# Four-layer conditional residual kernel on one core: W0 in four row quarters, added to and turned quarter by quarter

## What is computed

```
x = x + x @ W.T + ((x @ A[idx0].T) @ Bm[idx0].T) * scal[idx0]   # layer 0, a matrix and a rank-16 adapter per sequence
x = x + per-sequence mix of the tokens with w1[idx1]            # layer 1, 64 x 64
x = x + causal attention(x, beta = min(cond, 4)), 16 heads      # layer 2, Wq Wk Wv Wo
x = x + per-sequence mix of the tokens with w3[idx3]            # layer 3, 64 x 64
```

## Time and profile before

| | before |
|---|---|
| median of three runs | 611.03 us (610.99 to 611.15) |
| the profiled execution: time | 610.91 us |
| its span, first to last instruction | 609.2 us, 21490 instructions |
| TensorE busy | 601.7 us (99%) |
| VectorE busy | 392.9 us (64%) |
| ScalarE busy | 224.8 us (37%) |
| GpSimd busy | 109.8 us (18%) |
| mean granted TensorE clock | 0.997 |
| chain of work that ended last | PE 95%, DVE 4%, issue 1% |

### The profile page before, as it was taken

The page is one execution under the profiler, slowest core; times in us unless marked ns, Lnnn a source line. Parts: engine busy times, 40 slices in busy tenths (PEclk is TensorE's granted clock), DMA queues, the critical chain, the costliest instruction groups (busy, mean ns, idle before and its releaser), DMA issues.

```text
span 609.2 us, 21490 instructions
## 1 busy us (share of the span) xinstructions
PE 601.7 (99%) x8524; PEld 521.0 (86%) x8524; DVE 392.9 (64%) x573; ACT 224.8 (37%) x434; POOL 109.8 (18%) x101
## 2 busy tenths in 40 slices
PE   9999999899999999999999999999999999999998
PEld 8898889788898988889888898988889898888885
DVE  4699865665657567575775657567575766647374
ACT  4555351342524334251442424344251443513222
POOL 2003120301203031040401204040030302103030
PEclk9999999899999999999999999999999999999999
DMA  9962322222222322223222322322222231320212
GB/s 292 173 130 66 87 56 75 74 63 74 71 64 80 93 71 62 73 60 78 73 65 73 86 74 57 88 73 61 74 64 73 74 79 59 65 72 3 71 41 104
DMA packets 65272, 48.29 MB, mean 79 GB/s; under 512 B 16922, under 2 KB 51738, under 8 KB 65242
## 3 DMA queue, kind: packets, MB, share of 16 engines
q1 hardware_dynamic: 60090, 42.63, 26.7%
q10 hardware_dynamic: 5152, 5.24, 3.0%
HBM read 30.54 MB, written 17.30 MB: 79 GB/s over the span
## 4 chain that ended last, share of the span: by engine, by line
PE 95%; DVE 4%; issue 1%; ACT 0%; DVEq 0%; ACTq 0%
PE banks L654 10%; PE banks L649 10%; PE banks L650 10%; PE banks L748 5%; PE banks L677 5%; PE banks L749 5%; PE banks L755 5%; PE banks L681 5%; PE banks L679 5%; PE banks L589 4%; PE banks L591 4%; PE banks L593 4%; PE banks L702 4%; PE banks L694 4%; PE banks L718 3%; PE banks L616 3%
## 5 line engine op out<-in xcount | busy, mean ns | idle before, releaser
L649 PE MATMUL banks<-x1T_hi,w_hi 128*128 128x256 f32 x512 | 129.8, 286 | 0.0
L650 PE MATMUL banks<-x1T_hi,w_lo 128*128 128x256 f32 x512 | 128.3, 283 | 0.0
L649 PEld LDWEIGHTS banks<-x1T_hi,w_hi 128*128 128x128 f32 x512 | 98.1, 192 | 0.7 <-ACT x1T_hi L914 0.4
L650 PEld LDWEIGHTS banks<-x1T_hi,w_lo 128*128 128x128 f32 x512 | 98.2, 192 | 0.0
L654 PE MATMUL banks<-x1T_lo,w_hi 128*128 128x256 f32 x512 | 82.4, 283 | 0.1
L1428 POOL TENSOR_TENSOR probs<-probs,row_max 128x1024 f32<-128x1024 f32 x32 | 61.0, 1905 | 114.2 <-DVE row_max L1209 114.2
L1410 POOL TENSOR_TENSOR w_own<-w_in,own 128x128 f32<-128x128 f32 x32 | 14.8, 463 | 362.0 <-PE banks L616 265.9
L654 PEld LDWEIGHTS banks<-x1T_lo,w_hi 128*128 128x128 f32 x512 | 70.6, 192 | 0.4 <-DVE x1T_lo L1120 0.3
L1195 DVE TENSOR_TENSOR qkT<-banks,beta 128x512 f32<-128x512 f32 x32 | 22.1, 689 | 59.3 <-PE banks L654 59.3
L914 ACT ACTIVATE x_y<-banks 128x512 f32<-128x512 f32 (+1 forms) x17 | 9.9, 584 | 128.7 <-PE banks L616 122.0
L1213 DVE TENSOR_REDUCE row_sum<-probs 128x16 f32<-128x1024 f32 x32 | 39.0, 1218 | 24.5 <-ACT probs L996 24.5
(11 more groups left out here) (138 smaller groups left out, 1056.8 us busy)
## 6 DMA issues: line engine op xcount, KB each, us to landing
x_rows<-x_in SPq DMA_DIRECT2D x64, 128.0 KB, 2.4
x_kept<-x_rows SPq DMA_DIRECT2D x16, 512.0 KB, 3.6
x_in<-in_x_dram SPq DMA_DIRECT2D x60, 128.0 KB, 2.8
out_dram<-x_y SPq DMA_DIRECT2D x15, 512.0 KB, 3.0
b_sel<-b_parts SPq DMA_DIRECT2D x180, 32.0 KB, 1.7
w_in<-in_L_cond_weights_dram SPq DMA_DIRECT2D x128, 16.0 KB
probsT<-in_L_cond_W_dram ACTq DMA_DIRECT2D x1, 1024.0 KB, 6.1
probs<-in_L_cond_Wk_dram ACTq DMA_DIRECT2D x1, 1024.0 KB, 5.3
```

The costliest lines, as they stand in the source:

```text
L649: nc.tensor.matmul(out_ap, w_hi[:, w, c, cols], x1T_hi[:, c, :], start=(c == 0), stop=False)
L650: nc.tensor.matmul(out_ap, w_lo[:, w, c, cols], x1T_hi[:, c, :], start=False, stop=False)
```

## The change

W0 is loaded in four transfers, one for each 128 rows, each with a semaphore. The identity is added per row quarter: quarter n needs it only in columns n * 128 to n * 128 + 127. Two of the four additions stand ahead of the `xT_lo` operations on VectorE, the third between them and the fourth behind. TensorE turns by row quarter: quarter `oc` goes into groups 0 to 2 as soon as it has its addition, and group 3 follows as a whole, after `first_copied`. The three matmuls on zeros ahead of W0 are gone. Layer 0 of pair 0 now runs, for each c, the four products with `w_hi` behind `turned_hi` and then the two with `w_lo` behind `turned_lo`; before, all six stood behind `turned_lo`.

```diff
         def diagonal(n):
-            return bass.AP(tensor=probsT, offset=n, ap=[[HG * HEADS * S, P], [D + P, NC], [NC, P // NC]])
+            return stage[W0][:, n, n * P:(n + 1) * P]
...
             def turn_part(k, dc):
                 if dc == 0:
-                    if k != W0:
-                        pe.wait_ge(w_loaded[k], 16)
-                if k == W0:
-                    pe.wait_ge(diag_added, dc + 1)
+                    pe.wait_ge(w_loaded[k], 16)
                 turn(GROUPS_OF[k][dc], pieces_of(k, dc))
+
+
+            def turn_w0():
+                groups = GROUPS_OF[W0]
+                for oc in range(NC):
+                    pe.wait_ge(diag_added, oc + 1)
+                    for dc in range(NC - 1):
+                        turn_pieces(groups[dc], in_chunks(bank_of_group(groups[dc])), pieces_of(W0, dc), (oc,))
+                pe.wait_ge(first_copied, TILES)
+                turn_pieces(groups[-1], in_chunks(bank_of_group(groups[-1])), pieces_of(W0, NC - 1), range(NC))
...
+            def first_layer0_part(c):
+                pe.wait_ge(turned_hi, GROUPS_OF[W0][c] + 1)
+                for t in range(TILES):
+                    for x_part in (xT_hi, xT_lo):
+                        nc.tensor.matmul(bank[MIX[t]], x_part[:, c, tok(t)], w_hi[:, W0, c, :],
+                                         start=(c == 0 and x_part is xT_hi), stop=False)
+                pe.wait_ge(turned_lo, GROUPS_OF[W0][c] + 1)
+                for t in range(TILES):
+                    nc.tensor.matmul(bank[MIX[t]], xT_hi[:, c, tok(t)], w_lo[:, W0, c, :], start=False, stop=False)
...
             spread_rows()
-            stay_busy(3)
-            for c in range(NC):
-                if c == NC - 1:
-                    pe.wait_ge(first_copied, TILES)
-                turn_part(W0, c)
+            turn_w0()
...
             for c in range(NC):
-                pe.wait_ge(turned_lo, GROUPS_OF[W0][c] + 1)
-                for t in range(TILES):
-                    layer0_part(t, c)
+                first_layer0_part(c)
...
-            load_w(W0, W)
+            for n in range(NC):
+                act.dma_start(stage[W0][:, n, :], W[n * P:(n + 1) * P, :]).then_inc(w0_part_loaded[n], 16)
...
+            def add_identity(n):
+                dve.wait_ge(w0_part_loaded[n], 16)
+                nc.vector.tensor_tensor(diagonal(n), diagonal(n), ident[:], ALU.add).then_inc(diag_added, 1)
+
+            dve.wait_ge(ident_step, 2)
+            for n in range(2):
+                add_identity(n)
             for t in range(TILES):
                 dve.wait_ge(first_hi_done, t + 1)
                 rest(xT_lo[:, :, tok(t)], in_chunks(bank[SC[t]]), xT_hi[:, :, tok(t)]).then_inc(first_lo_done, 1)
-
-
-            dve.wait_ge(ident_step, 2)
-            dve.wait_ge(w_loaded[W0], 16)
-            for n in range(NC):
-                columns = ident[:].rearrange("p (e c) -> p c e", c=NC)[:, n, :]
-                nc.vector.tensor_tensor(diagonal(n), diagonal(n),
-                                        columns.unsqueeze(1).to_broadcast([P, NC, P // NC]), ALU.add)\
-                    .then_inc(diag_added, 1)
+                add_identity(2 + t)
```

More of the change, by code:

```diff
@@ L187, in cond_resid_kernel @@
         w_loaded = [sem(f"w_loaded{k}") for k in range(NW)]
+        w0_part_loaded = [sem(f"w0_part_loaded{n}") for n in range(NC)]
         x_first_loaded = sem("x_first_loaded")
```

## The result

| | before | after |
|---|---|---|
| median, 6 runs each on one chip | 610.81 us (609.02 to 611.15) | 613.30 us (610.66 to 614.32) |
| ratio after / before | | 1.0043, 95% interval 1.0025 to 1.0062 |
| the profiled execution: time, span | 610.91, 609.2 us | 610.66, 608.9 us |
| its mean granted TensorE clock | 0.997 | 1.000 |
| TensorE waiting for "issue" inside `scores` | 1.6 us, once | 2.8 us, twice |

The prediction was 610.96 us, within 610.4 to 611.9. The measured 613.3 is outside it, and the interval of the ratio leaves out "no change".

What follows compares the result with a forecast made beforehand. TensorE bounds the kernel, tied in the prologue with the chain to `a_all`: 0.87 us saved becomes 0.09, put at 0.07 for the start from idle; 610.91 less 0.07 is 610.84, median 0.12 above: 610.96 us, range 610.4 to 611.9.

Steps and rivals of the forecast that it cites:

- Others: Side effects on SyncE's load of Wv and TensorE's instruction count; the 1.58 us stall at 107.32 us should stay.
- The stall at 107 us moves: Rival: this TensorE stall disappears, down to 608.2 us, or a larger or second one costs as much, 613.8; 6%, half each.
- 1.2 us per fall: Cost of a TensorE clock fall at the 107 us stall: six products 0.2 us slower each.
- The 0.87 us of TensorE's saving become 0.09: Prologue: the adapter product waits for `a_all`, so it starts at 12.51 instead of 12.60 us.
- The 0.05 us for starting from idle: At the adapter product, starting from idle may cost the overlap of load and matmul, some 0.05 us.
- the cover: Prologue: all waits that the change adds or moves are covered, by 0.3 to 0.4 us.
- The quarters land together: Rival: W0's quarters all land at 7.4 us, delaying `xT_lo` and the first `w_hi` by 1.0 us; 612.0 us, 6%.
- a quarter-size transfer in a filled queue keeps the full rate: Rule for W0's load: quarters land 0.8 us apart, without the fixed DMA cost of about 2 us paid each time.
- used up exactly: ScalarE's queue: three more issues of 0.54 us end the table load at 5.79 us, using all 1.61 us of cover before `xT_hi`.
- the two rivals at 611.9: W0's quarters landing together, 612.0 us, and the TensorE clock falling in the prologue, 611.9 us; 6% each.

Runs made afterwards that it cites:

- e1: The changed kernel with 13 already-met waits put back on TensorE ahead of the adapter product; 610.88 us, ratio 0.9998.
- e5: The changed kernel with only 6 already-met TensorE instructions put back instead of 13; 610.37 us, ratio 0.9998.
- e7: The changed kernel with A copied right behind W0's group 0, in another bank, and 13 met TensorE waits added; 610.58 us, ratio 0.9998.
- e8: The changed kernel with the three matmuls on zeros kept ahead of W0, 12 of the 13 instructions; 610.17 us, ratio 0.9998.
- e9: The changed kernel, TensorE's program untouched, with VectorE scaling the first half of q ahead of turning x for pair 3; 609.53 us, ratio 0.9997.
- e10: The changed kernel without padding, A copied behind W0's group 0, x for pair 3 turned at the end of VectorE's step 0; 610.22 us, ratio 0.9994.
- e2: The kernel before without the three matmuls on zeros, 12 TensorE instructions fewer, W0 still in one transfer; 612.83 us, ratio 1.0038.
- e3: The changed kernel with the 512 KB `x_kept` load of pair 0 held until the scores of pair 1 are done; 611.88 us, ratio 1.0019.
- e4: The kernel before with the `x_kept` load of pair 0 issued one gather sooner, TensorE's program untouched; 610.47 us, ratio 0.9997.
- e11: Control: the kernel before with VectorE scaling the first half of q ahead of turning x for pair 3; 609.53 us, ratio 0.9994.
- e6: The changed kernel run again, unedited, in the second batch on another chip; 614.06 us, ratio 1.0051.

## Why the prediction was wrong

**The step that failed** is in "Others": "TensorE's program gets shorter by six instructions and longer by four waits", and "a shift of a few instructions among hundreds should leave it". The count was off (13 shorter), and the conclusion too. A fetch was asked 48 to 52 instructions behind a seam, the wait for `q_scaled` stood 59 behind it, and the change moved it to 46. e1, e5, e7 and e8 (the numbering restored) and e9 and e10 (the wait let go earlier) take the stall away, e2 makes it in the kernel before, and e3, e4 and e11 leave the fetch as it was. The rival "The stall at 107 us moves" had the size right, "a larger or second one costs as much, 613.8", against 613.3 measured, but had 3% for it. The stall at 107 us did not move in any of the kernels; a second one came at 71 us, where the earlier trace rows did not look. That the old stall had no releaser in the profile should have made it a question about the instruction queue.

**The sum by what was measured:** 1.39 us of stall, and 0.74 more falls at 1.6 us, 1.2 us; less 0.1 us from the prologue: 2.5 us, as measured. That it fits so well is in part luck, since the number of falls rests on twelve runs: with 1.0 falls in the six runs of the result the sum is 1.9 us against 2.5 measured, with 1.67 in those of e6 3.0 against 3.2. The prediction's 1.2 us per fall was 0.4 too small.

**Point by point:**
- W0 from 7.45 us (7.49), first `w_hi` 9.01 (8.99), adapter product 12.51 (12.49), `a_all` as releaser, TensorE idle 0.5 us: right. "The 0.87 us of TensorE's saving become 0.09" measured 0.11 between the two traces. The agreement to 0.02 us is luck: the product starts at 11.87 (e6) and 11.93 us (e9) in other executions with the same prologue and at 12.87 in e3, and at 12.35 (e4) and 12.32 us (e11) with that of the kernel before, by when x is turned and when the quarters land. The 0.05 us for starting from idle did not show: the first product behind it starts at 14.13 instead of 14.24 us.
- Additions take 0.28 to 0.29 us: right. The second started at 6.27 us, not near 5.9, so that quarter landed about 0.4 us later than worked out. `xT_lo` slid by 0.07 us only; in this execution the cover held, barely. In e3 and e10 it did not, and the rival "The quarters land together" came true by half: the first `w_hi` 0.4 and 0.5 us late. So "a quarter-size transfer in a filled queue keeps the full rate" held in seven of the nine traces with quarters.
- Issues of the quarters: 0.49 us each, not 0.54, so the table load ended at 5.49 instead of 5.79 us and the cover that was to be "used up exactly" kept 0.3 us.
- SyncE reached the load of Wv at 10.23 us, 1.1 us sooner than before, which the prediction did not see; it is still behind the last piece of W0.
- The clock in the prologue: W0's 16 transposes in 2.00 us, at the upper level, without the three matmuls on zeros that stood ahead of them. The rule of the Trainium skill, "TensorE: Matmul & The Clock Gate", section "Part 4: PE-mode transpose", that transposes don't count as work for the gate, shows no cost in the kernel after. e2 shows what does go wrong there: 1.45 us of idling ahead of W0, then a granted clock of 0.57 from 8 to 12 us. With W0 in one transfer the zeros had filled most of that time; with quarters W0's first pieces fill it.
- The range took its upper end from the two rivals at 611.9 and left the second stall out as 3%. With 1.58 us of unexplained stall in the trace, that was too little.

**What stays open:** what in TensorE asks for a piece, and why a wait holds the request, is inferred from the places and not seen. Why the second quarter landed at 6.9 to 7.0 us in two executions and at 6.0 to 6.3 in the others isn't known. And whether the stall at 107 us can be taken away. There `attend` and `scores` follow each other without a break, 256 instructions in about 1.5 us, and from a seam to the use of the piece asked for behind it e9's trace shows 3.24 us (104.74 to 107.98). Filling the gap there might cost something in every pass of the loop; it wasn't tried.

## What to carry to other kernels

An engine's wait with "issue" as its releaser, inside a dense run of small instructions, is a question about the instruction queue: look for its transfers in the stretch and for a wait that was holding the engine when the next one was due. When an edit adds or drops instructions, even a dozen and far away, compare the places of such stalls in the two traces before believing any other reason; an edit with met waits of the same number tells the two apart in one run. And shorten the wait that holds the fetch (another engine's order), rather than tune the number: that survives the next edit.

## What the runs showed that was not expected

- TensorE's program comes in 16 KB pieces of 256 instructions; the one needed at 71 us is asked for 48 to 52 instructions behind a seam. The transfer takes 0.9 to 2.1 us over the 13 traces, and TensorE resumes 1.2 to 1.5 us behind its end.
- Data traffic did not lengthen the fetch by anything that mattered: 1.09 us beside data transfers with a share of 23.4% (kernel after), 1.20 us alone on the queues (e3).
- A run of 64 products of 32 x 64 takes 0.9 us, and attention's products are quicker still, so one piece lasts TensorE about 1.5 us there, less than a fetch takes from request to use. Two stalls of that kind are 0.5% of this kernel's time, and each comes with a chance of a 1.6 us fall of the clock.
